# Third feed-forward: ScalarE rounds the gelu rows, VectorE takes the low part a unit later, the down projection stands three units behind

## The chip, the cores and the metric

The kernel runs on one core of one Trainium2 chip. The metric is the device time of one execution in microseconds (us). PE is the matmul engine TensorE, PEld its weight loads, DVE is VectorE, ACT is ScalarE, POOL is GpSimd, SP is the engine that issues the DMAs.

## The reference

`x` has 64 batches of 128 tokens with 128 features. Four layers follow one another; each adds a cross-attention to a context (16 heads) and then a feed-forward. The change touches the third feed-forward alone, a mixture of 8 experts with capacity, cut here to what is computed:

```python
scores = softmax(xt @ wg); gvals, gidx = top_k(scores, 2)        # 8 experts
gvals = gvals / sum(gvals); keep = (place of the token in its expert's queue) < cap
h = gelu(einsum('ecd,edh->ech', disp, w1) + b1[:, None, :])      # D=128 -> H=512
y = einsum('ech,ehd->ecd', h, w2) + b2[:, None, :]
out = sum over the two experts of y * gval * keep
```

The kernel works it out densely: every token goes through all 8 experts, and each expert's output is multiplied by the token's gate, which is zero where the token isn't routed to it or is over the capacity. 8 experts of 512 hidden features are 32 blocks of 128.

## The kernel before

`gated_outputs_phase` is used twice: with kind "capacity" for the third feed-forward (tiles named f2 in the code; the profile leaves numbers out and writes f_a, f_ah and so on) and with kind "swiglu" for the fourth (f3). The flag `two` is true for the fourth.

The 8192 tokens are worked in 16 groups of 512. In a group there is one unit for each hidden block: N = 32 units in the third feed-forward, so 512 units in the stage. fp32 products are made of three passes over operands split in a high part (fp32r, rounded) and a low part (the rest): high x high, low weight x high, high weight x low. One unit n consists of

- up (TensorE): three 128x512 matmuls of the split inputs `XH`, `XL` into `PU[n % 2]`, counted by `up_ready`. It waits until the gelu of unit n-2 is done (`a_ready` at n-1).
- rows (ScalarE): gelu with bias from `PU` into `A[n % 2]`, counted by `a_ready`. It waits for `up_ready` and for `lo_ready` at n-1, that is for the low part of unit n-2, the last reader of the `A` buffer that it overwrites.
- high: `AH[n % 4]` = `A` rounded to fp32r, counted by `hi_ready`. In the third feed-forward VectorE does it (line 1642), in the fourth ScalarE (line 1734).
- low (VectorE, line 1648): `AL[n % 4]` = `A` - `AH`, counted by `lo_ready`. It waits for `hi_ready` of its own unit.
- down (TensorE): three matmuls of `AH` and `AL` into `PY`, which gathers the four units of an expert. The first unit of an expert also has one bf16 matmul (line 1794) that spreads the gates into `PG`.

For each expert ScalarE copies `PG` to SBUF (spread, line 1749), VectorE weighs the expert's output with it (weigh, line 1663, after the down of the expert's fourth unit), and GpSimd sums the weighed outputs in SBUF (lines 1608 and 1611, 7 sums in a group). Once in a group TensorE turns the sum back and VectorE adds it to `x` and takes statistics (finish, in unit 5), TensorE and ScalarE bring the next group's gates in (unit 8), and VectorE splits the next group's inputs (unit 10, lines 1627 and 1629).

The order on every engine is written out by hand: the `group` function of each engine lists what it does in unit s. `lagged(g, s, first, lag, f)` calls f for the unit that lies `lag` units back, in the group before if need be. The down projection, weigh and spread lie LAG units back; LAG is 2 in the third feed-forward and 3 in the fourth. Engines run their own list in order and meet at semaphores only. The first and the last groups are written out, the others are a loop of two groups (`groups_loop`).

Of the kernel before, what the change touches and what calls it, by code (L numbers as in the profile page):

```python
# [39 lines left out]
def at_least(eng, sem, value):  # L40

    if isinstance(value, int) and value <= 0:
        return
    eng.wait_ge(sem, value)
# [1453 lines left out]
def gated_outputs_phase(nc, R, I, name, kind, out=None):  # L1498
# [7 lines left out]
    HB = 4 if kind == "capacity" else 2  # L1506
    N = E * HB
    two = kind == "swiglu"
    LAG = 3 if two else 2


    SUM_UNIT, TURN_UNIT, SPLIT_UNIT, PRESUM_UNIT = 5, 8, 10, 12
# [2 lines left out]
    with ExitStack() as stack:  # L1515
# [41 lines left out]
        def lagged(g, s, first, lag, f):  # L1557

            if s >= lag:
                f(g, s - lag)  # L1560
            elif not first:
                f(g - 1, N + s - lag)

        with nc.Block() as block:
# [56 lines left out]
            @block.vector  # L1621
            def _(dve):
                v = nc.vector
                def split_inputs(g, par):
                    src = X.ht[:, bass.ds(g * GT, GT)]
                    at_least(dve, Z["up_ready"], (g - 1) * N)
                    v.tensor_copy(XH[par][:], src).then_inc(Z["xh_ready"], 1)
                    dve.wait_ge(Z["xh_ready"], g + 1)
                    v.tensor_tensor(XL[par][:], src, XH[par][:].bitcast(F32), ALU.subtract).then_inc(Z["xl_ready"], 1)

                def product(g, s):
                    n = g * N + s
                    dve.wait_ge(Z["s_ready"], n + 1)
                    dve.wait_ge(Z["up_ready"], n + 1)
                    at_least(dve, Z["lo_ready"], n - 1)
                    v.tensor_tensor(A[s % 2][:], S[s % 2][:], PV[s % 2][:], ALU.mult).then_inc(Z["a_ready"], 1)  # L1636

                def high(g, s):
                    n = g * N + s
                    dve.wait_ge(Z["a_ready"], n + 1)  # L1640
                    at_least(dve, Z["dn_ready"], n - 3)
                    v.tensor_copy(AH[s % 4][:], A[s % 2][:]).then_inc(Z["hi_ready"], 1)  # L1642

                def low(g, s):
                    n = g * N + s
                    dve.wait_ge(Z["hi_ready"], n + 1)
                    at_least(dve, Z["dn_ready"], n - 3)
                    v.tensor_tensor(AL[s % 4][:], A[s % 2][:], AH[s % 4][:].bitcast(F32),  # L1648
                                    ALU.subtract).then_inc(Z["lo_ready"], 1)

                def weigh(g, u):

                    if u % HB != HB - 1:
                        return
                    e = u // HB
                    dve.wait_ge(Z["gx_ready"], g * E + e + 1)
                    dve.wait_ge(Z["dn_ready"], g * N + u + 1)

                    at_least(dve, Z["ya_ready"], g * ADDS + (e - 1 if e < 2 else max(1, e - 2)))
                    if two:  # L1660
                        ins = v.tensor_tensor(YG[e % 2][:], PY[e % 2][:], GX[e % 2][:], ALU.mult)  # L1661
                    else:
                        ins = v.scalar_tensor_tensor(YG[e % 2][:], PY[e % 2][:], B2[:, e:e + 1], GX[e % 2][:], ALU.add, ALU.mult)  # L1663
                    ins.then_inc(Z["yg_ready"], 1)

                def presum(g, par):

                    dve.wait_ge(kept_in[par], ctx_count(g, par))
                    v.tensor_tensor(KEPT[par][:], KEPT[par][:], R.x[:, bass.ds(g * GB, GB), :],
                                    ALU.add).then_inc(Z["presummed"], 1)  # L1670

                def group(g, par, first, last):
                    for s in range(N):
                        if out is not None and s == PRESUM_UNIT:
                            presum(g, par)
                        if two:
                            product(g, s)
                            lagged(g, s, first, 1, low)
                        else:
                            high(g, s)  # L1680
                            low(g, s)
                        lagged(g, s, first, LAG, weigh)
                        if s == SUM_UNIT and not first:
                            finish(g - 1, 1 - par)
                        if s == SPLIT_UNIT and not last:
                            split_inputs(g + 1, 1 - par)
                    if last:
                        if two:
                            low(g, N - 1)
                        for u in range(N - LAG, N):  # L1690
                            weigh(g, u)
                        finish(g, par)

                def finish(g, par):

                    dve.wait_ge(Z["px_ready"], g + 1)
                    if out is not None:
                        dve.wait_ge(Z["presummed"], g + 1)
                        v.tensor_tensor(KEPT[par][:], KEPT[par][:], PT[:], ALU.add).then_inc(Z["x_added"], 1)
                        return  # L1700
                    residual(nc, R, dve, Z["x_added"], g, PT[:], g + 1)

                split_inputs(0, 0)

                v.tensor_copy(g3[:, :, 0, :], X.gates[:]).then_inc(Z["split"], 1)
                dve.wait_ge(Z["split"], 1)
                v.tensor_tensor(rest[:], X.gates[:], g3[:, :, 0, :], ALU.subtract).then_inc(Z["split"], 1)
                dve.wait_ge(Z["split"], 2)
                v.tensor_copy(g3[:, :, 1, :], rest[:]).then_inc(Z["split"], 1)
                dve.wait_ge(Z["split"], 3)  # L1710
                v.tensor_tensor(rest[:], rest[:], g3[:, :, 1, :], ALU.subtract).then_inc(Z["split"], 1)
                dve.wait_ge(Z["split"], 4)
                v.tensor_copy(g3[:, :, 2, :], rest[:]).then_inc(Z["split"], 1)
                groups_loop(dve, group)

            @block.scalar
            def _(act):
                a = nc.scalar

                def rows(g, s):  # L1720
                    n = g * N + s
                    act.wait_ge(Z["up_ready"], n + 1)
                    if two:
                        at_least(act, Z["a_ready"], n - 1)
                        a.activation(S[s % 2][:], PU[s % 2][:], ACT.Silu).then_inc(Z["s_ready"], 1)  # L1725
                    else:
                        at_least(act, Z["lo_ready"], n - 1)
                        a.activation(A[s % 2][:], PU[s % 2][:], ACT.Gelu, bias=B1[:, s:s + 1]).then_inc(Z["a_ready"], 1)  # L1728

                def high(g, s):  # L1730
                    n = g * N + s
                    act.wait_ge(Z["a_ready"], n + 1)
                    at_least(act, Z["dn_ready"], n - 3)
                    a.activation(AH[s % 4][:], A[s % 2][:], ACT.Copy).then_inc(Z["hi_ready"], 1)

                def gates_in(g, par):
                    act.wait_ge(Z["gt_psum"], g + 1)
                    at_least(act, Z["ge_ready"], (g - 1) * E)
                    a.activation(G3T[par][:], PT[0:K3, :, :].rearrange("p b t -> p (b t)"),
                                 ACT.Copy).then_inc(Z["gt_ready"], 1)  # L1740

                def spread(g, u):

                    if u % HB != 0:
                        return
                    e = u // HB
                    act.wait_ge(Z["ge_ready"], g * E + e + 1)
                    at_least(act, Z["yg_ready"], g * E + e - 1)
                    a.activation(GX[e % 2][:], PG[:], ACT.Copy).then_inc(Z["gx_ready"], 1)

                def group(g, par, first, last):
                    for s in range(N):
                        rows(g, s)
                        if two:
                            lagged(g, s, first, 1, high)
                        lagged(g, s, first, LAG, spread)
                        if s == TURN_UNIT and not last:
                            gates_in(g + 1, 1 - par)
                    if last:
                        if two:  # L1760
                            high(g, N - 1)
                        for u in range(N - LAG, N):
                            spread(g, u)

                gates_in(0, 0)
                groups_loop(act, group)
# [187 lines left out]
```

## Time and profile before

| | us |
|---|---|
| median of 3 runs (4551.13 to 4552.9) | 4552.88 |
| span of the profiled execution, first to last instruction | 4550.5 |
| TensorE busy in it | 4085.3 |
| VectorE busy | 3902.8 |
| ScalarE busy | 2713.1 |
| GpSimd busy | 1476.4 |

The profiled execution has no other time of its own on record than its span; it lies 2.4 us under the median of the timed runs. The third feed-forward is the stretch from about 1995 us to 2812 us. Its steady part, 2050 to 2750 us, holds TensorE at full granted clock. A matmul's busy time overlaps that of the next one, since they are pipelined: their starts, not their durations, give the cadence. Instructions of VectorE and ScalarE that don't depend on each other also overlap by about 0.1 us.

### The profile page before, as it was taken

What the parts mean: (1) busy time and instruction counts of PE and PEld (TensorE: products, weight loads), DVE (VectorE), ACT (ScalarE), POOL (GpSimd) and SP (SyncE); (2) the same over time, 40 slices, a digit from 0 to 9 for tenths busy, and PEclk for the clock granted to TensorE, in tenths of its full rate; (3) what the DMA queues carried; (4) which work ended last, traced back from release to release, by engine and by line L of the source; (5) the groups of instructions that cost most, each with busy time, mean ns of one, the idle gap of its engine ahead of it and who ended that gap; (6) DMA issues with size and microseconds to landing.
All of it is one profiled execution on the core that took longest, in us unless ns stands there. A gap on an engine that the chain in (4) does not pass through costs nothing. (4 is left out here: it accounts for less than half of the span.)

```text
span 4550.5 us, 105158 instructions
## 1 busy us (share of the span) xinstructions
PE 4085.3 (90%) x34134; PEld 2858.5 (63%) x34135; DVE 3902.8 (86%) x7025; ACT 2713.1 (60%) x4836; POOL 1476.4 (32%) x779
## 2 busy tenths in 40 slices
PE   6984789994997999869999997999949999699999
PEld 3562556664774666657777775666636666577777
DVE  7888789997996888779999998888868888688888
ACT  3433577772775777535555554777757777366665
POOL 2210055540004555312111213555525555122222
PEclk9976999995998999869999998999969999699999
DMA  1010022221002222200000000222222221100000
GB/s 59 17 46 1 11 68 63 65 49 49 1 0 57 57 59 58 78 24 1 1 0 1 0 1 23 64 55 60 52 64 47 55 50 47 72 15 14 14 14 14
DMA packets 129636, 162.04 MB, mean 36 GB/s; under 512 B 32972, under 2 KB 88593, under 8 KB 128306
## 3 DMA queue, kind: packets, MB, share of 16 engines
q1 hardware_dynamic: 129457, 159.97, 13.3%
q8 instruction: 75, 1.23, 0.1%
q14 instruction: 104, 0.84, 0.1%
HBM read 36.38 MB, written 8.39 MB: 10 GB/s over the span
## 5 line engine op out<-in xcount | busy, mean ns | idle before, releaser
L709 ACT ACTIVATE a_p<-a_p 128x480 f32<-128x480 f32 x832 | 500.7, 602 | 408.0 <-DVE a_p L551 403.8
L1648 DVE TENSOR_TENSOR f_al<-f_a,f_ah 128x512 fp32r<-128x512 f32 x768 | 690.9, 900 | 17.5
L347 POOL TENSOR_TENSOR a_km<-a_k,a_slots 96x1920 fp32r<-96x1920 f32 x186 | 631.8, 3416 | 180.8 <-DMA a_k<-a_kh 180.8
L546 DVE TENSOR_REDUCE a_mx<-a_sc 128x4 f32<-128x480 f32 (+1 forms) x832 | 543.0, 653 | 140.0 <-PE a_sc L802 108.2
L1728 ACT ACTIVATE f_a<-f_pu,f_b 128x512 f32<-128x512 f32 x512 | 353.4, 690 | 374.1 <-PE f_pu L1231 198.6
L551 DVE TENSOR_TENSOR a_p<-a_sc,a_mx 128x480 f32<-128x480 f32 x832 | 531.8, 639 | 18.8
L715 ACT ACTIVATE a_pt<-a_tp 120x512 f32<-120x512 f32 x832 | 486.4, 585 | 76.3 <-PE a_tp L811 73.8
L811 PE MATMUL a_tp<-ident,a_p 128*120 128x128 f32 x3328 | 511.8, 276 | 12.0 <-ACT a_p L709 9.7
L1611 POOL TENSOR_TENSOR f_ya<-f_ya,f_yg 128x512 f32<-128x512 f32 x192 | 254.0, 1323 | 769.1 <-DVE f_yg L1663 466.6
L811 PEld LDWEIGHTS a_tp<-ident,a_p 128*120 128x120 f32 x3328 | 400.3, 138 | 98.8 <-ACT a_p L709 34.8
L796 PE MATMUL a_sc<-a_km,a_qr 96*128 96x480 f32 x768 | 396.2, 516 | 33.0 <-ACT a_qr L704 31.4
L1227 PE MATMUL f_py<-f_ah,f_wdhi 128*128 128x512 f32 x768 | 355.2, 462 | 3.0 <-DVE f_ah L1642 3.0
L835 PE MATMUL a_nd<-a_pt,a_vm 120*32 120x128 f32 x6656 | 354.9, 285 | 0.0
L835 PE MATMUL a_nd<-a_pt,a_dm 120*32 120x128 f32 x6656 | 334.4, 273 | 0.0
L1231 PE MATMUL f_py<-f_al,f_wdhi 128*128 128x512 f32 x768 | 312.6, 407 | 6.2 <-DVE f_al L1648 4.4
L1227 PE MATMUL f_pu<-f_xh,f_w1hi 128*128 128x512 f32 x768 | 310.8, 405 | 3.6 <-DVE f_a L1636 3.5
L1228 PE MATMUL f_py<-f_ah,f_wdlo 128*128 128x512 f32 x768 | 303.3, 395 | 0.0
L1228 PE MATMUL f_pu<-f_xh,f_w1lo 128*128 128x512 f32 x768 | 303.2, 395 | 0.0
L1231 PE MATMUL f_pu<-f_xl,f_w1hi 128*128 128x512 f32 x768 | 302.6, 394 | 0.0
L1725 ACT ACTIVATE f_s<-f_pu 128x512 f32<-128x512 f32 x256 | 153.5, 600 | 212.6 <-PE f_pv L1231 212.6
L559 DVE RECIPROCAL a_rd<-a_nd 128x128 f32<-128x128 f32 x256 | 242.8, 948 | 6.7 <-PE a_nd L835 6.5
L347 POOL TENSOR_TENSOR s_km<-s_k,s_slots 96x2048 fp32r<-96x2048 f32 x62 | 223.9, 3631 | 53.0 <-DMA s_k<-s_kh 53.0
(403 smaller groups left out, 9394.3 us busy)
## 6 DMA issues: line engine op xcount, KB each, us to landing
a_q<-a_qh SPq DMA_DIRECT2D x384, 64.0 KB, 2.0
a_k<-a_kh SPq DMA_DIRECT2D x384, 60.0 KB, 2.0
a_ctx<-in_ctxT SPq DMA_DIRECT2D x64, 240.0 KB, 2.7
a_q<-a_ql SPq DMA_DIRECT2D x192, 64.0 KB, 2.0
a_k<-a_kl SPq DMA_DIRECT2D x192, 60.0 KB, 2.0
s_k<-s_kh SPq DMA_DIRECT2D x128, 64.0 KB, 2.0
s_q<-s_qh SPq DMA_DIRECT2D x128, 64.0 KB, 2.0
x<-in_x SPq DMA_DIRECT2D x4, 1024.0 KB, 7.9
```

The costliest lines, as they stand in the source:

```text
L347: v.tensor_tensor(KM[par][:, i, :, :].rearrange("p b (j k) -> p b j k", k=KN), K3[:, i, :, :].unsqueeze(2).to_broadcast([TR, GB, 4, KN]), ...
L546: v.tensor_reduce(mx[:], view, AX.X, ALU.max).then_inc(mx_ready, 1)
L551: v.tensor_tensor(PR[s % 4][:].rearrange("p (h k) -> p h k", k=k), view, mx[:].unsqueeze(2).to_broadcast([P, heads, k]), ALU.subtract).the ...
L709: a.activation(PR[s % 4][:], PR[s % 4][:], ACT.Exp).then_inc(exp_ready, 1)
L715: a.activation(PT[s % 4][0:KN, :], TP[s % 2][0:KN, :], ACT.Copy).then_inc(pt_ready, 1)
L796: last = t.matmul(SC[s % 2][:, 0:W], queries, keys, start=True, stop=not masked)
L811: last = t.transpose(TP[s % 2][0:KN, q * P:(q + 1) * P], PR[s % 4][:, q * KN:(q + 1) * KN], R.ident[:])
L835: last = t.matmul(ND[j % 2][32 * q:32 * q + 32, what, :], w, PT[s % 4][0:KN, q * P:(q + 1) * P], start=(what == 0 and i == 0), stop=(i == ...
L1227: t.matmul(out, w_hi, a_hi, start=start, stop=False)
L1228: t.matmul(out, w_lo, a_hi, start=False, stop=False)
L1231: return t.matmul(out, w_hi, a_lo, start=False, stop=stop)
L1648: v.tensor_tensor(AL[s % 4][:], A[s % 2][:], AH[s % 4][:].bitcast(F32), ALU.subtract).then_inc(Z["lo_ready"], 1)
```

## The change

In the third feed-forward the high part is taken by ScalarE, one unit after the gelu, in place of VectorE; the low part on VectorE moves one unit back; and LAG becomes 3, so down, weigh and spread lie three units back. The conditions on semaphores stay as they are, and so do the numbers of buffers: `A` has 2, `AH` and `AL` have 4. The fourth feed-forward had this order already.

```diff
--- before.py
+++ after.py
@@ -1506,7 +1506,7 @@
     HB = 4 if kind == "capacity" else 2
     N = E * HB
     two = kind == "swiglu"
-    LAG = 3 if two else 2
+    LAG = 3
 
 
     SUM_UNIT, TURN_UNIT, SPLIT_UNIT, PRESUM_UNIT = 5, 8, 10, 12
@@ -1635,12 +1635,6 @@
                     at_least(dve, Z["lo_ready"], n - 1)
                     v.tensor_tensor(A[s % 2][:], S[s % 2][:], PV[s % 2][:], ALU.mult).then_inc(Z["a_ready"], 1)
 
-                def high(g, s):
-                    n = g * N + s
-                    dve.wait_ge(Z["a_ready"], n + 1)
-                    at_least(dve, Z["dn_ready"], n - 3)
-                    v.tensor_copy(AH[s % 4][:], A[s % 2][:]).then_inc(Z["hi_ready"], 1)
-
                 def low(g, s):
                     n = g * N + s
                     dve.wait_ge(Z["hi_ready"], n + 1)
@@ -1675,18 +1669,14 @@
                             presum(g, par)
                         if two:
                             product(g, s)
-                            lagged(g, s, first, 1, low)
-                        else:
-                            high(g, s)
-                            low(g, s)
+                        lagged(g, s, first, 1, low)
                         lagged(g, s, first, LAG, weigh)
                         if s == SUM_UNIT and not first:
                             finish(g - 1, 1 - par)
                         if s == SPLIT_UNIT and not last:
                             split_inputs(g + 1, 1 - par)
                     if last:
-                        if two:
-                            low(g, N - 1)
+                        low(g, N - 1)
                         for u in range(N - LAG, N):
                             weigh(g, u)
                         finish(g, par)
@@ -1751,14 +1741,12 @@
                 def group(g, par, first, last):
                     for s in range(N):
                         rows(g, s)
-                        if two:
-                            lagged(g, s, first, 1, high)
+                        lagged(g, s, first, 1, high)
                         lagged(g, s, first, LAG, spread)
                         if s == TURN_UNIT and not last:
                             gates_in(g + 1, 1 - par)
                     if last:
-                        if two:
-                            high(g, N - 1)
+                        high(g, N - 1)
                         for u in range(N - LAG, N):
                             spread(g, u)
```

How the instructions stand. On ScalarE at the start of the stage, before (f2_a0 and f2_a1 are the two buffers of gelu rows, f2_pu the up projection's, f2_gx the spread gates):

```order
L1728 ACTIVATE f2_a0<-f2_pu0,f2_b1 128x512
L1728 ACTIVATE f2_a1<-f2_pu1,f2_b1 128x512
L1728 ACTIVATE f2_a0<-f2_pu0,f2_b1 128x512
L1749 ACTIVATE f2_gx0<-f2_pg 128x512
L1728 ACTIVATE f2_a1<-f2_pu1,f2_b1 128x512
L1728 ACTIVATE f2_a0<-f2_pu0,f2_b1 128x512
L1728 ACTIVATE f2_a1<-f2_pu1,f2_b1 128x512
L1728 ACTIVATE f2_a0<-f2_pu0,f2_b1 128x512
```

and in the changed kernel (f2_ah0 to f2_ah3 are the high parts):

```order
L1718 ACTIVATE f2_a0<-f2_pu0,f2_b1 128x512
L1718 ACTIVATE f2_a1<-f2_pu1,f2_b1 128x512
L1724 ACTIVATE f2_ah0<-f2_a0 128x512
L1718 ACTIVATE f2_a0<-f2_pu0,f2_b1 128x512
L1724 ACTIVATE f2_ah1<-f2_a1 128x512
L1718 ACTIVATE f2_a1<-f2_pu1,f2_b1 128x512
L1724 ACTIVATE f2_ah2<-f2_a0 128x512
L1739 ACTIVATE f2_gx0<-f2_pg 128x512
L1718 ACTIVATE f2_a0<-f2_pu0,f2_b1 128x512
L1724 ACTIVATE f2_ah3<-f2_a1 128x512
```

After the first two gelus each gelu has the rounding of the unit before behind it: the gelu into f2_a0 of unit 2 now stands right behind the rounding that reads f2_a0 of unit 0.

On VectorE at the same place, before (f2_al are the low parts, f2_yg the weighed output):

```order
L1642 CAST f2_ah2<-f2_a0 128x512
L1648 TENSOR_TENSOR f2_al2<-f2_a0,f2_ah2 128x512
L1642 CAST f2_ah3<-f2_a1 128x512
L1648 TENSOR_TENSOR f2_al3<-f2_a1,f2_ah3 128x512
L1642 CAST f2_ah0<-f2_a0 128x512
L1648 TENSOR_TENSOR f2_al0<-f2_a0,f2_ah0 128x512
L1642 CAST f2_ah1<-f2_a1 128x512
L1648 TENSOR_TENSOR f2_al1<-f2_a1,f2_ah1 128x512
L1663 SCALAR_TENSOR_TENSOR f2_yg0<-f2_py0,f2_b2,f2_gx0 128x512
L1642 CAST f2_ah2<-f2_a0 128x512
```

and in the changed kernel:

```order
L1642 TENSOR_TENSOR f2_al2<-f2_a0,f2_ah2 128x512
L1642 TENSOR_TENSOR f2_al3<-f2_a1,f2_ah3 128x512
L1642 TENSOR_TENSOR f2_al0<-f2_a0,f2_ah0 128x512
L1642 TENSOR_TENSOR f2_al1<-f2_a1,f2_ah1 128x512
L1657 SCALAR_TENSOR_TENSOR f2_yg0<-f2_py0,f2_b2,f2_gx0 128x512
L1642 TENSOR_TENSOR f2_al2<-f2_a0,f2_ah2 128x512
```

The casts are gone from VectorE, and between two weighings four low parts are left; the weighing of expert 0 comes one unit later.

## Rows read from the trace of the kernel before

**Rows 1.** the page, part 1: busy us, share of span, x instructions
```profile
PE 4085.3 (90%) x34134; PEld 2858.5 (63%) x34135; DVE 3902.8 (86%) x7025; ACT 2713.1 (60%) x4836; POOL 1476.4 (32%) x779
```

**Rows 2.** busy time by engine in a steady stretch of the changed stage
```profile
core 0: us, PE busy (x) PEld busy (x) DVE busy (x) ACT busy (x) POOL busy (x), PEclk, DMA share, GB/s
2050.00:2750.00 700.00, 682.26 (x2881) 501.90 (x2880) 662.75 (x1097) 368.08 (x568) 138.25 (x110) 1.00 0.00 1
```

**Rows 3.** groups by line, same stretch: busy us, mean ns, idle before, releaser
```profile
L1648 DVE TENSOR_TENSOR f_al<-f_a,f_ah 128x512 fp32r<-128x512 f32 x444 | 400.9, 903 | 15.2
L1728 ACT ACTIVATE f_a<-f_pu,f_b 128x512 f32<-128x512 f32 x443 | 305.8, 690 | 329.2 <-PE f_pu L1231 169.2 <-DVE f_al L1648 158.1
...
L1642 DVE CAST f_ah<-f_a 128x512 fp32r<-128x512 f32 x444 | 187.6, 423 | 19.5 <-issue 14.8 <-ACT f_a L1728 4.5
...
L1611 POOL TENSOR_TENSOR f_ya<-f_ya,f_yg 128x512 f32<-128x512 f32 x82 | 109.7, 1338 | 403.9 <-DVE f_yg L1663 403.9
```

**Rows 4.** who waited for whom, same stretch: us total, times, longest
```profile
ACT f_a L1728 <- DVE f_al L1648: 158.1, 130, 2.9
...
PEld f_py L1231 <- DVE f_al L1648: 43.3, 124, 1.1
```

**Rows 5.** timeline of ACT, the stage's first and last gelu instructions
```profile
2000.77 1.28 ACT L1728 ACT_TABLE_LOAD   x1
2002.07 1.34 ACT L1728 ACTIVATE f_a<-f_pu,f_b 128x512 f32<-128x512 f32 x2
...
2803.85 0.69 ACT L1728 ACTIVATE f_a<-f_pu,f_b 128x512 f32<-128x512 f32 x1 [0.46 <-PE f_pu L1231]
```

**Rows 6.** timeline, DVE, ACT and POOL around one sum of outputs
```profile
2305.31 0.69 ACT L1728 ACTIVATE f_a<-f_pu,f_b 128x512 f32<-128x512 f32 x1 [0.71 <-PE f_pu L1231]
...
2305.79 0.75 DVE L1663 SCALAR_TENSOR_TENSOR f_yg<-f_py,f_b,f_gx 128x512 f32<-128x512 f32 x1
...
2305.90 0.59 ACT L1749 ACTIVATE f_gx<-f_pg 128x512 f32<-128x512 f32 x1
...
2306.45 0.42 DVE L1642 CAST f_ah<-f_a 128x512 fp32r<-128x512 f32 x1
...
2306.70 1.32 POOL L1611 TENSOR_TENSOR f_ya<-f_ya,f_yg 128x512 f32<-128x512 f32 x1 [4.63 <-DVE f_yg L1663]
...
2306.91 1.67 DVE L1648 TENSOR_TENSOR f_al<-f_a,f_ah 128x512 fp32r<-128x512 f32 x1
...
2308.67 0.69 ACT L1728 ACTIVATE f_a<-f_pu,f_b 128x512 f32<-128x512 f32 x1 [1.04 <-DVE f_al L1648]
...
2309.01 0.69 DVE L1648 TENSOR_TENSOR f_al<-f_a,f_ah 128x512 fp32r<-128x512 f32 x1
...
2309.62 0.42 DVE L1642 CAST f_ah<-f_a 128x512 fp32r<-128x512 f32 x1
```

**Rows 7.** groups by line, the fourth feed-forward: ScalarE's rounding
```profile
L1734 ACT ACTIVATE f_ah<-f_a 128x512 fp32r<-128x512 f32 x256 | 159.6, 623 | 3.8 <-DVE f_a L1636 3.8
```

**Rows 8.** timeline, a VectorE instruction released by ScalarE
```profile
2317.03 0.69 ACT L1728 ACTIVATE f_a<-f_pu,f_b 128x512 f32<-128x512 f32 x1
...
2317.75 0.43 DVE L1642 CAST f_ah<-f_a 128x512 fp32r<-128x512 f32 x1 [0.32 <-ACT f_a L1728]
```

**Rows 9.** timeline of PE, the cadence of back-to-back matmuls
```profile
2304.42 0.39 PE L1227 MATMUL f_pu<-f_xh,f_w1hi 128*128 128x512 f32 x1
2304.65 0.40 PE L1228 MATMUL f_pu<-f_xh,f_w1lo 128*128 128x512 f32 x1
```

**Rows 10.** timeline of DVE, residual and statistics, then the next unit
```profile
2312.41 0.68 DVE L154 TENSOR_TENSOR x<-x,f_pt 128x512 f32 x1
...
2314.16 0.41 DVE L1642 CAST f_ah<-f_a 128x512 fp32r<-128x512 f32 x1
```

**Rows 11.** PE busy us and granted clock, 1 us stretches, first attention
```profile
180.00:181.00 1.00, 0.00 (x0) 1.00 0.00 0
182.00:183.00 1.00, 1.00 (x5) 0.50 0.00 0
```

## The prediction

> **What bounds the kernel now.** I read the page's sum first, then the busy times of the stage that changes, its groups by line, its waits, and last a few microseconds of its timeline. The page shows TensorE busy for 90% of the span and VectorE for 86% [rows 1]; that is a mean over all stages. In 700 us of the third feed-forward TensorE is busy 682.26 us and VectorE 662.75 us, both nearly full, ScalarE only 368.08 us, at full granted clock [rows 2]. One VectorE unit is a cast of 423 ns and a low part of 903 ns on average [rows 3]; one TensorE unit is six matmuls that start 0.23 us apart, 1.40 us [rows 9]. The pace of the stage: the first gelu starts at 2002.07, the last, 511 units later, at 2803.85 [rows 5], so 801.8 us, or 1.57 us a unit. TensorE is the bound most of the time, and its weight load for the low part's pass waits 43.3 us in all for VectorE [rows 4]. By busy shares alone, moving a cast from a 95% engine to a 53% engine looks like a gain. What decides is another row: already now the gelu (ScalarE, line 1728) stands idle 158.1 us, 130 times, until a low part is done [rows 4]. The gelu of unit n may not overwrite `A[n % 2]` before the low part of unit n-2 has been taken from it, since there are two `A` buffers. That wait stays, and the change lengthens what hangs on it.
>
> **The change, part by part.**
>
> The cast leaves VectorE: 512 casts of 423 ns, 217 us of work [rows 3]. A rounding of the same size enters ScalarE; the fourth feed-forward has that instruction at 623 ns [rows 7], 319 us of work. As load this would fit: ScalarE would have 0.59 us for the gelu (0.69 less 0.10 of overlap), 0.52 for the rounding (0.62 less the same), and a spread for every fourth unit.
>
> The ring is the point. ScalarE's list is now gelu n, rounding n-1, gelu n+1, rounding n, and so on. Gelu n+1 waits for low part n-1, low part n-1 waits for rounding n-1, and rounding n-1 stands on ScalarE directly ahead of gelu n+1. Nothing of the low part can lie beside ScalarE's work any more except a spread. Before, cast and low part of unit n-1 both ran on VectorE while ScalarE was free to do gelu n. So one unit of the changed kernel is this chain, in order:
>
> - gelu starts, the next independent instruction on ScalarE starts 0.59 us later (2305.31 to 2305.90) [rows 6];
> - the rounding, 0.62 us [rows 7];
> - from ScalarE's end to VectorE's start 0.03 us (2317.03 + 0.69 to 2317.75) [rows 8];
> - the low part, 0.69 us when nothing blocks it (the row at 2309.01) [rows 6];
> - from its end to the gelu's start 0.09 us (2306.91 + 1.67 = 2308.58 to 2308.67) [rows 6].
>
> Together 2.02 us, with the unrounded 623 and 693 ns 2.03 us. The spread hides: it starts 0.5 us after the rounding's start and lasts 0.59, while rounding, hop and low part take 1.34. TensorE hides wholly: it needs 1.40 us a unit (and a little for the gates), it may start up n+2 once gelu n is done, and down stands three units back, so nobody waits for it. LAG 3 therefore buys nothing here and costs nothing: on VectorE a weighing starts right behind a low part, 0.61 us after that low part's start (2309.01 to 2309.62) [rows 6], and is over before ScalarE has done gelu and rounding.
>
> The GpSimd sums. After a weighing GpSimd sums SBUF tiles for 1.32 us, beginning 0.91 us after the weighing began (2305.79 to 2306.70); the low part that meets it lasts 1.67 us in place of 0.69 and ends 0.56 us after the sum's end (2308.02 to 2308.58) [rows 6]. In the new order, with t the start of the low part ahead of the weighing: weighing t+0.61, sum t+1.52 to t+2.84, next low part ready at t+2.03 and done at t+2.84+0.56 = t+3.40 rather than t+2.72. So each sum costs the ring 0.68 us. There are 7 in each of 16 groups, 112. Bounds: nothing, if the low part came first and the sum had to wait; 0.98 us each (1.67 - 0.69), if the whole lengthening of the row shows. I take 0.68, being the arithmetic of the same rows with the new distances.
>
> The Trainium skill ("SBUF — State Buffer", "Who interferes with whom") says that a VectorE instruction with two SBUF inputs contends with a GpSimd instruction that reads SBUF, and that ScalarE never waits on anyone. The trace agrees with the first part: 1.67 against 0.69 us [rows 6]. By that rule the rounding on ScalarE is safe from the sums, and the low part stays exposed.
>
> Once a group. Finish in unit 5 holds VectorE for 1.75 us (2312.41 to 2314.16) [rows 10]; it starts at t+0.61, so the next low part starts at t+2.36 and not t+2.03: 0.33 us, 15 times. The split of inputs in unit 10 now stands behind a weighing, because LAG 3 brings one there: cast and subtraction follow it, the subtraction meets the GpSimd sum, and the low part behind it ends about 0.6 us later than a plain blocked one (its own 0.69, overlapped by 0.09), 15 times. No table is loaded again: the only ACT_TABLE_LOAD here is at the start of the stage [rows 5], though gelus and copies alternate already.
>
> The stage's end: before, two whole downs were left behind the last gelu, now part of three, but the weighing waits for the last low part in both; I cost it at nothing.
>
> The sum: 511 x 2.03 = 1037.3; 112 x 0.68 = 76.2; 15 x 0.33 = 5.0; 15 x 0.6 = 9.0; together 1127.5 us against 801.8 now, that is +325.7 us. The span of 4550.5 becomes 4876.2, and the profiled execution lies 2.4 us under the median of the timed runs, so on the median of 4552.88 the forecast is 4878 us, 7.2% slower.
>
> **The rivals.**
>
> *Slow clock in the gaps.* TensorE will work 1.40 us and stand for 0.63 us in every unit (1.3 us where a sum blocks). If the granted clock falls to its lower level in such gaps, a unit of matmuls costs up to 2.8 us, more than the ring's mean of 1127.5 / 511 = 2.21 us. For it: in the first attention TensorE idles from 180 to 181 us with the clock at 1.00, and from 182 to 183 us, busy again, it has 0.50 [rows 11]. Against it: the gaps here are mostly shorter than that whole idle microsecond, and at the low clock TensorE would have no gap left, so that it would be busy throughout and the clock could not stay down. At worst I let half the units run so: 256 x (2.8 - 2.21) = 151, 5029 us. The Trainium skill ("TensorE: Matmul & The Clock Gate", "A second HAM failure mode: psum-queue depth-cycling") holds that micro-idles between matmul groups make the clock swing between its levels; that speaks for this rival, and no stretch of this trace has such short gaps in every unit to test it.
>
> *Faster: relief of VectorE wins.* Then a unit would go at TensorE's pace. For it: the 95% busy VectorE, and the 43.3 us for which TensorE's weight loads wait [rows 2, 4]. The price: at most 43.3 x 809 / 700 = 50 us, for 809 us of stage, giving 4503; at least the 17.74 us that TensorE is idle in 700, so 20. The point from which it decides is the ring's length: it must be under 1.57 us, and that needs a gelu which doesn't wait for the low part behind the rounding just issued. Two rows alone, rounding 0.62 and low part 0.69, with 0.59 for the gelu, are already 1.90.
>
> *The sums block longer.* All of 0.98 us each: 112 x 0.30 = 34 more, 4912. *The sums don't block:* 76 less, 4802. The row at 1.67 speaks against the second.
>
> *Smaller handovers.* 0.03 us from VectorE to ScalarE in place of 0.09: 31 less, 4847.
>
> **How the numbers follow.** The ring holds with a chance of 0.96: 0.76 near my sum, 0.08 with longer blocks, 0.05 with no blocks or smaller handovers, 0.07 with the clock falling often enough to be seen. Relief of VectorE gets 0.03, no difference 0.01. The range, 4835 to 4930, reaches from a little below the smaller handovers to above the longer blocks with a few falls of the clock. A measurement of this kernel tells 0.2%, 9 us, from no change: slower 0.96, same 0.01, faster 0.03.
>
> **What would show it.** Right: the gelu's wait for the low part rises from 158 us to most of ScalarE's idle time and happens in nearly every unit; gelu starts 2.03 us apart, about 2.7 behind a sum; the rounding at 0.62 us; waits of TensorE are for the gelu, no longer for the low part; the stage lasts some 1135 us with TensorE busy about two thirds, at granted clock 1.0; all other stages unchanged. Wrong: gelu starts less than 1.57 us apart (the ring isn't one), a granted clock under 1.0 inside the stage, or low parts that last 0.69 us in every unit (the sums don't block).

## The result, and the profile after

The changed kernel takes 4873.81 us (median, 4869.67 to 4874.8) against 4552.62 us: ratio 1.0705, 95% interval 1.0692 to 1.0718. The forecast was 4878, in a range of 4835 to 4930. The profiled execution took 4869.67 us, the shortest of the four, so what follows from the trace is about 4 us less than the medians say.

Part 1 of the page of the changed kernel, beside [rows 1]:

```profile
PE 4241.6 (87%) x34134; PEld 2832.8 (58%) x34135; DVE 3686.0 (76%) x6513; ACT 2974.6 (61%) x5348; POOL 1470.9 (30%) x779
```

VectorE has 512 instructions less and 217 us less work, as counted; ScalarE has 512 more and 262 us more work. VectorE lost load and the time went up all the same, so VectorE's load is not what sets it; that ScalarE's isn't either is shown by e1 and e9 below. The stage that changed, in a steady stretch, beside [rows 2], and the fourth feed-forward, which has the same order and didn't change:

```profile
core 0: us, PE busy (x) PEld busy (x) DVE busy (x) ACT busy (x) POOL busy (x), PEclk, DMA share, GB/s
2050.00:3050.00 1000.00, 841.17 (x2958) 493.55 (x2957) 489.94 (x666) 611.31 (x1039) 138.97 (x114) 1.00 0.00 0
2005.00:3120.00 1115.00, 938.75 (x3299) 550.57 (x3297) 544.53 (x741) 682.29 (x1159) 152.49 (x124) 1.00 0.00 0
4300.00:4800.00 500.00, 496.74 (x2215) 386.11 (x2214) 439.53 (x610) 311.26 (x568) 135.69 (x111) 1.00 0.05 14
```

VectorE falls from 95% to 49% busy, TensorE from 97% to 84% by records that overlap (by starts it has 1.40 us of matmuls in 2.19 us, 64%), and the clock is granted in full. In the fourth feed-forward (last row) TensorE stays full with the rounding in the same place: there ScalarE's activation goes to a buffer `S` of its own, which is free once VectorE's product has read it, ahead of the rounding and not behind it. That reason is read from the code; no run tests it. The groups by line of the same 1000 us, beside [rows 3] (busy us, mean ns, then idle time before them and its releaser):

```profile
L1642 DVE TENSOR_TENSOR f_al<-f_a,f_ah 128x512 fp32r<-128x512 f32 x455 | 367.1, 807 | 506.7 <-ACT f_ah L1724 506.7
L1718 ACT ACTIVATE f_a<-f_pu,f_b 128x512 f32<-128x512 f32 x455 | 312.7, 687 | 388.7 <-DVE f_al L1642 388.7
L1724 ACT ACTIVATE f_ah<-f_a 128x512 fp32r<-128x512 f32 x456 | 283.4, 621 | 0.0
...
L1611 POOL TENSOR_TENSOR f_ya<-f_ya,f_yg 128x512 f32<-128x512 f32 x86 | 111.0, 1290 | 650.4 <-DVE f_yg L1657 650.4
```

Each of the 455 gelus now waits for a low part, and 427 of the 455 low parts wait for a rounding: the two idle columns, 388.7 and 506.7 us, are the two halves of the ring. The rounding itself never waits. The waits of the same stretch, beside [rows 4]:

```profile
ACT f_a L1718 <- DVE f_al L1642: 388.7, 455, 1.6
PEld f_pu L1227 <- ACT f_a L1718: 245.8, 420, 0.6
...
PEld f_py L1231 <- DVE f_al L1642: 159.8, 334, 1.5
```

TensorE's weight loads wait for the gelu 420 times, and for the low part 334 times. One of these gaps, in its timeline:

```profile
2307.49 0.47 PE L1231 MATMUL f_py<-f_al,f_wdhi 128*128 128x512 f32 x1
2308.24 0.50 PE L1227 MATMUL f_pu<-f_xh,f_w1hi 128*128 128x512 f32 x1 [0.28 <-ACT f_a L1718]
```

Matmuls otherwise start 0.23 us apart, so about 0.5 us of this unit is empty. The ring itself, in the timeline of ScalarE and VectorE (start us, duration us, engine, line):

```profile
2307.51 0.69 ACT L1718 ACTIVATE f_a<-f_pu,f_b 128x512 f32<-128x512 f32 x1 [0.82 <-DVE f_al L1642]
2308.09 0.62 ACT L1724 ACTIVATE f_ah<-f_a 128x512 fp32r<-128x512 f32 x1
2309.53 0.69 ACT L1718 ACTIVATE f_a<-f_pu,f_b 128x512 f32<-128x512 f32 x1 [0.82 <-DVE f_al L1642]
2310.12 0.62 ACT L1724 ACTIVATE f_ah<-f_a 128x512 fp32r<-128x512 f32 x1
2311.56 0.69 ACT L1718 ACTIVATE f_a<-f_pu,f_b 128x512 f32<-128x512 f32 x1 [0.82 <-DVE f_al L1642]
...
2314.23 0.69 ACT L1718 ACTIVATE f_a<-f_pu,f_b 128x512 f32<-128x512 f32 x1 [0.98 <-DVE f_al L1642]
```

```profile
2308.74 0.69 DVE L1642 TENSOR_TENSOR f_al<-f_a,f_ah 128x512 fp32r<-128x512 f32 x1 [1.33 <-ACT f_ah L1724]
2310.77 0.69 DVE L1642 TENSOR_TENSOR f_al<-f_a,f_ah 128x512 fp32r<-128x512 f32 x1 [1.33 <-ACT f_ah L1724]
2311.38 0.74 DVE L1657 SCALAR_TENSOR_TENSOR f_yg<-f_py,f_b,f_gx 128x512 f32<-128x512 f32 x1
2312.80 1.34 DVE L1642 TENSOR_TENSOR f_al<-f_a,f_ah 128x512 fp32r<-128x512 f32 x1 [0.67 <-ACT f_ah L1724]
```

```profile
2312.29 1.29 POOL L1611 TENSOR_TENSOR f_ya<-f_ya,f_yg 128x512 f32<-128x512 f32 x1 [8.06 <-DVE f_yg L1657]
```

Gelu at 2307.51, rounding 0.58 us later at 2308.09, its end at 2308.71, low part from 2308.74 to 2309.43, next gelu at 2309.53: 2.02 us, link by link as forecast. At 2311.56 the same chain meets a GpSimd sum: the low part lasts 1.34 us, and the next gelu comes after 2.67 us.

### The profile page after: what moved, and what is told of

Its sections match the earlier page's. It is cut to its first block and busy times, and to the rows that moved or that the text cites. A ratio compares the mean times of both kernels' runs of the same rounds, so it can differ in the third digit from the quotient of the medians.

```text
span 4867.9 us, 105172 instructions
## 1 busy us (share of the span) xinstructions
PE 4241.6 (87%) x34134; PEld 2832.8 (58%) x34135; DVE 3686.0 (76%) x6513; ACT 2974.6 (61%) x5348; POOL 1470.9 (30%) x779
## 5 line engine op out<-in xcount | busy, mean ns | idle before, releaser
L1642 DVE TENSOR_TENSOR f_al<-f_a,f_ah 128x512 fp32r<-128x512 f32 x768 | 641.4, 835 | 575.1 <-ACT f_ah L1724 575.1
L1724 ACT ACTIVATE f_ah<-f_a 128x512 fp32r<-128x512 f32 x768 | 477.8, 622 | 3.9 <-DVE f_a L1636 3.9
L1227 PE MATMUL f_pu<-f_xh,f_w1hi 128*128 128x512 f32 x768 | 360.4, 469 | 120.3 <-ACT f_a L1718 102.8
L1231 PE MATMUL f_py<-f_al,f_wdhi 128*128 128x512 f32 x768 | 335.2, 436 | 59.5 <-DVE f_al L1642 57.7
L1227 PEld LDWEIGHTS f_pu<-f_xh,f_w1hi 128*128 128x128 f32 x768 | 144.2, 188 | 303.2 <-ACT f_a L1718 276.1
```

The lines of the kernel that those rows point to most:

```text
L1227: t.matmul(out, w_hi, a_hi, start=start, stop=False)
L1231: return t.matmul(out, w_hi, a_lo, start=False, stop=stop)
```

## The experiments

All edits are in the third feed-forward only, and the diffs show the lines that matter; `...` stands for lines left out. Times are medians, and ratios are to the kernel before on the same chip. It took 4552.09 to 4552.99 us on all of them, so the runs can also be held against the changed kernel's 4873.81.

**Cut the ring: four buffers of gelu rows (e1).**

```diff
-        A = [sb(n_(f"a{i}"), [P, GT]) for i in range(2)]
+        NA = 2 if two else 4
+        A = [sb(n_(f"a{i}"), [P, GT]) for i in range(NA)]
...
-                        at_least(act, Z["lo_ready"], n - 1)
+                        at_least(act, Z["lo_ready"], n - NA + 1)
...
```

> The changed kernel with four buffers of gelu rows instead of two, so that the gelu of unit n waits for the low part of unit n-4 and not of unit n-2; the order on every engine is the changed one. Ring theory: the chain gelu, rounding, low part, gelu is cut, ScalarE needs 0.59 + 0.52 + 0.5/4 = 1.24 us a unit, VectorE about 1.15, TensorE 1.40 and its gates, so TensorE sets the pace: about 4505 us, between 4495 and 4540. Rival, ScalarE's own load is what costs: stays near 4870. Rival, LAG 3 or the clock in the gaps: stays above 4800.

Measured 4535.62 us, ratio 0.9967 (0.9954 to 0.9979): within the range given, 31 us over the 4505 expected. With ScalarE's and VectorE's lists unchanged, 338 us come back for two buffers. The groups by line of 650 us of the stage:

```profile
L1719 ACT ACTIVATE f_a<-f_pu,f_b 128x512 f32<-128x512 f32 x420 | 289.6, 690 | 93.3 <-PE f_pu L1231 70.2 <-issue 20.6
L1725 ACT ACTIVATE f_ah<-f_a 128x512 fp32r<-128x512 f32 x420 | 261.1, 622 | 0.0
```

The gelu's idle time is now for TensorE, except for 20.6 us "issue", to which the last two runs return. ScalarE's load is as in the changed kernel, so it was not the load.

**Cut the ring by order alone: rounding behind its own gelu (e4).** Two buffers, three units behind; ScalarE's list is gelu n, rounding n, and VectorE takes the low part of unit n in its own step.

```diff
-                        lagged(g, s, first, 1, high)
+                        lagged(g, s, first, 1 if two else 0, high)
...
-                        lagged(g, s, first, 1, low)
+                        lagged(g, s, first, 1 if two else 0, low)
```

> The changed kernel, still two buffers and ScalarE rounding, but the rounding stands right behind the gelu of its own unit and the low part is not put back a unit. Ring theory: the low part of unit n-1 now runs beside gelu and rounding of unit n, so ScalarE needs about 0.72 + 0.52 + 0.5/4 = 1.37 us a unit and TensorE sets the pace: 4500 to 4540 us. Rival, ScalarE's load costs: no better than 4870. Rival, LAG 3: above 4800.

Measured 4510.92 us, ratio 0.9911 (0.9894 to 0.9927), the fastest of all and faster than both kernels. In it the low part of unit n-1 has all of gelu and rounding n to run beside. Busy times of 650 us of the stage:

```profile
2050.00:2700.00 650.00, 650.00 (x2840) 505.48 (x2839) 415.71 (x643) 607.83 (x996) 163.53 (x110) 1.00 0.00 0
```

TensorE has no idle in the records; the gelu's starts put a group at 47.67 us (759.1 us for 511 units, 1.49 a unit), 1.40 us of matmuls a unit and the gates' and transposes' share. As far as the records show, the order of the other engines has nothing more to give here.

**LAG alone, both ways (e2, e3).** e2 is the changed kernel with `LAG = 3 if two else 2`; e3 is the kernel before with `LAG = 3`.

> The changed kernel with down projection, weighing and spread two units behind instead of three. Ring theory: the ring is the same, 2.03 us a unit; only the split of inputs no longer stands behind a weighing, 15 times 0.6 = 9 us less: about 4865 us. Rival, three units behind is what costs: back near 4553 us.

> The kernel before with the down projection, weighing and spread three units behind instead of two, rounding still on VectorE. Ring theory: nothing is in the ring that was not there; TensorE's waits for the low part (43 us in 700) shrink, the split of inputs meets a GpSimd sum: 4520 to 4560 us. Rival, three units behind is what costs: above 4800 us.

Measured 4869.66 us for e2 (ratio to before 1.07, 1.0682 to 1.0718) and 4538.8 us for e3 (0.9972, 0.9961 to 0.9983). Three units behind costs nothing; in the kernel before it gains 13 us. The waits of e3 in 650 us:

```profile
ACT f_a L1728 <- DVE f_al L1648: 292.4, 314, 2.9
...
PEld f_py L1231 <- DVE f_al L1648: 5.6, 13, 0.4
```

TensorE waits 5.6 us for the low part, where the kernel before has 40.5 in the same 650 us. Not all of the gain is this. By the gelu starts the stage is 14 us shorter: most groups last 49.0 us and not 49.5, and in every other group VectorE's idle at the top of its loop (see the last two runs) falls from 2.5 to 1.4 us, which gives 6 of the 14.

e2 lies 4 us under the changed kernel where 9 were expected, and by its gelu starts only 0.8 us (1118.0 against 1118.8). The unit with the split of inputs is back at 2.02 us and the sum there costs the unit before it its 0.6 us, so the split gives back the expected 0.7 us a group; but now finish stands behind a weighing and its unit takes 2.98 us in place of 2.33, which takes the same away.

**One link shortened: half a low part (e8).** The subtraction covers 256 of 512 columns; the other half of `AL` is written once at the start.

```diff
-                    v.tensor_tensor(AL[s % 4][:], A[s % 2][:], AH[s % 4][:].bitcast(F32),
+                    W = GT if two else 256
+                    v.tensor_tensor(AL[s % 4][:, 0:W], A[s % 2][:, 0:W], AH[s % 4][:, 0:W].bitcast(F32),
...
```

> The changed kernel whose low part in the third feed-forward covers 256 of the 512 columns (the other half keeps what was written once at the start), all else as it is. Ring theory: the low part is a link of the ring, so its shortening by an estimated 0.27 us (from 0.69) comes back in each of 512 units: 137 us less, about 4737 us. Rival, the cost is ScalarE's load or TensorE's gaps: VectorE is idle half the time already, so no change, 4874.

Measured 4736.62 us (ratio 1.041, 1.0393 to 1.0427), 137 us under the changed kernel. One instruction of an engine that is idle half the time became 0.27 us shorter, and every unit with it. Its timeline:

```profile
2304.64 0.69 ACT L1723 ACTIVATE f_a<-f_pu,f_b 128x512 f32<-128x512 f32 x1 [0.55 <-PE f_pu L1231]
...
2306.40 0.69 ACT L1723 ACTIVATE f_a<-f_pu,f_b 128x512 f32<-128x512 f32 x1 [0.55 <-DVE f_al L1643]
```

```profile
2305.88 0.42 DVE L1643 TENSOR_TENSOR f_al<-f_a,f_ah 128x256 fp32r<-128x256 f32 x1 [1.33 <-ACT f_ah L1729]
```

1.76 us from gelu to gelu, with a low part of 0.42 us.

**Work beside the ring shortened: a spread of 64 columns (e9).**

```diff
-                    a.activation(GX[e % 2][:], PG[:], ACT.Copy).then_inc(Z["gx_ready"], 1)
+                    W = GT if two else 64
+                    a.activation(GX[e % 2][:, 0:W], PG[:, 0:W], ACT.Copy).then_inc(Z["gx_ready"], 1)
...
```

> The changed kernel whose spread on ScalarE covers 64 of 512 columns (the rest keeps what was written once), so that ScalarE has about 0.4 us less work in 128 places, 50 us. Ring theory: the spread lies beside rounding and low part, so nothing comes back: 4874, within 9. Rival, ScalarE's load is what costs: 40 to 50 us less, about 4828.

Measured 4872.43 us (1.0707, 1.0689 to 1.0725). The spread lasts 0.21 us in place of 0.59 in 128 places, and nothing comes back:

```profile
L1740 ACT ACTIVATE f_gx<-f_pg 128x64 f32<-128x64 f32 x74 | 15.9, 214 | 0.0
```

e8 and e9 are the pair that tells a ring from a load: the instruction on the less busy engine counted in full, the one on the busier engine not at all.

**The sums: 64 of 512 columns (e5).** Both additions of GpSimd on `YA[par][:, 0:64]`.

> The changed kernel whose GpSimd sums in the third feed-forward cover 64 of 512 columns, so that they last a small part of 1.3 us. Ring theory with blocking: 112 units lose their 0.62 us, and the split of inputs its 0.6, 15 times: 78 us less, about 4796 us. If the sums don't block the low part: 4874.

Measured 4796.75 us (1.0538, 1.052 to 1.0555): 77 us less by the medians, 72 by the gelu starts of the two traces (1046.6 against 1118.8). The low part and the sum:

```profile
L1644 DVE TENSOR_TENSOR f_al<-f_a,f_ah 128x512 fp32r<-128x512 f32 x317 | 219.2, 692 | 352.2 <-ACT f_ah L1726 352.2
...
L1613 POOL TENSOR_TENSOR f_ya<-f_ya,f_yg 128x64 f32<-128x64 f32 x59 | 18.9, 320 | 463.3 <-DVE f_yg L1659 463.3
```

The mean low part is 692 ns, where the changed kernel has 807; none is blocked any more.

**The kernel before with four buffers (e6).** The edit of e1, with the cast left on VectorE.

> The kernel before with four buffers of gelu rows, rounding still on VectorE and down two units behind. In the kernel before the gelu waited 158 us in 700 for a low part, but TensorE waited only 43 us for VectorE, and VectorE is 95% busy: the gelu's waits go, VectorE's load stays. Expected 4545 us, between 4520 and 4555. If the gelu's wait was what held TensorE: 4505.

Measured 4553.42 us (1.0003, 0.9993 to 1.0013): no change. The gelu's waits for the low part are gone from its trace and have become waits for TensorE (289.2 us, 398 times, in 650); TensorE's own wait for the low part is the old one:

```profile
ACT f_a L1729 <- PE f_pu L1231: 289.2, 398, 1.6
...
PEld f_py L1231 <- DVE f_al L1649: 41.0, 115, 1.1
```

So two buffers were enough for the old order. With ScalarE rounding they are enough too, if the rounding stands right behind its own gelu (e4); they are too few when it stands a unit later, directly ahead of the gelu that waits for its low part.

**The top of the loop (e10, e11).** In e1 every other group lasted 51.7 us by its gelu starts, the others 47.5. The gelu at the top of ScalarE's loop of two groups starts late, with no releaser:

```profile
2144.10 0.59 ACT L1740 ACTIVATE f_gx<-f_pg 128x512 f32<-128x512 f32 x1
2148.30 0.69 ACT L1719 ACTIVATE f_a<-f_pu,f_b 128x512 f32<-128x512 f32 x1 [3.62 <-issue]
```

e10 is e1 with ScalarE's list written out for 16 groups, e11 the kernel before with VectorE's list written out:

```diff
-                groups_loop(act, group)
+                if two:
+                    groups_loop(act, group)
+                else:
+                    for g in range(NG):
+                        group(g, g % 2, g == 0, g == NG - 1)
```

> The kernel with four buffers of gelu rows (run e1), with ScalarE's list of the third feed-forward written out for all 16 groups instead of a loop of two groups; the other engines keep their loops. In run e1 ScalarE stood 3.3 to 3.6 us with no releaser at the top of its loop, once per two groups, and every other group lasted 51.7 us in place of 47.5. If the jump back is what costs: 6 or 7 times 4 us, 25 us less, about 4511 us, as run e4. If it is something else in that place, such as the wait for a group's first inputs: 4535 us as before.

> The kernel before with VectorE's list of the third feed-forward written out for all 16 groups. In its trace every other group lasts 52.0 us in place of 49.5, and VectorE has six idles without a releaser, 14.8 us in 700. If the jump back costs: 6 or 7 times 2.5 us, about 17 us less, 4536 us. If not: 4552 us.

Measured 4522.12 us for e10 (0.9935, 0.9921 to 0.9948) and 4533.12 us for e11 (0.9957, 0.9943 to 0.997). The idles are gone in both, and every group of e10 but the first and the last lasts 48.3 us. e11 gains 20 us where 17 were expected. e10 gains 13 of 25 (17 by the gelu starts), because 25 was too much to expect: the groups of 47.5 us in e1 were not undisturbed ones but followed a stall, of which they made up 0.8 us. An undisturbed group lasts 48.3 us in e1 too (its second), so six jumps cost 2.5 us each, 15 in all. What still parts e10 from e4 is a smaller wait once in each group, TensorE's for a low part. e1 has it too, e4 doesn't:

```profile
PEld f_py L1231 <- DVE f_al L1643: 11.9, 14, 0.9
```

A group of e10 lasts 0.67 us more than one of e4, 11 us in all. The loop alone doesn't make the stall: ScalarE runs the same loop of two groups in the changed kernel and in e4, and has no such idle in either. Its longest there are 1.61 us and 1.08 us, both behind the split of inputs and for a low part.

## Why the prediction was right

*The ring.* Right, and shown from three sides: cut by buffers (e1), cut by order (e4), shortened in one link (e8, 137 us returned of 137 expected). The unit without a sum takes 2.02 to 2.03 us from gelu to gelu; the forecast was 2.03.

*The sums.* Sized 0.68 us; the gelu starts show 0.61 on average, mostly 0.64 and in the first and last groups 0.55. 0.03 of the difference is the sum's own length, now 1290 ns and not 1320. The forecast also charged 112 sums, where two come after the last gelu. e5 gives the whole term: 72 us by the gelu starts (77 by the medians) where 78 were expected of the split and 112 sums; of the split's 0.64 us only half came back.

*Once a group.* The unit of finish takes 2.33 us on average (+0.30; forecast +0.33), the unit behind the split of inputs 3.29 us (+0.64 over a blocked one; forecast +0.6).

*The sum.* From the first gelu at 2000.94 to the last at 3119.75 there are 1118.8 us, forecast 1127.5. The sums account for the 8.7 us: 110 at 0.61 make 67 and not 76. The ring's 2.025 us in place of 2.03 take 2 more off; against them stand 3 us that the forecast doesn't have, since the first three units of a group take 0.04 to 0.08 us longer, for a cause that stays open. On the medians the forecast is 4 us over. That so many small terms come out within a few us of each other is in part luck; that the ring makes up 1035 of 1118.8 us is not.

*LAG 3 costs and buys nothing.* The cost was right (e2, e3), and nobody waits for the down projection in the trace. One detail failed: TensorE was to wait for the gelu and no longer for the low part. It waits for both: TensorE runs two units ahead of ScalarE, so three units behind its own up projection is one unit behind the gelu, and the third pass comes just as the low part ends. It costs nothing, because the ring sets the pace. In the order of the kernel before LAG 3 would have been worth 13 us (e3). And the sign "TensorE busy about two thirds" holds by the starts of its matmuls (64%), not by the profile's busy share, which was 84%.

*The clock.* The rival with the lower clock didn't happen: TensorE stood about 0.5 us in a unit, longer behind a sum, and the granted clock was 1.00 from 2005 to 3120 us. What the Trainium skill says under "A second HAM failure mode: psum-queue depth-cycling", in "TensorE: Matmul & The Clock Gate", that frequent micro-idles between groups of matmuls make the clock swing, isn't borne out here.

*Relief of VectorE.* The rival had the right price for the wrong kernel: 4503 forecast for TensorE's pace, 4510.92 measured in e4, where the rounding on ScalarE is kept and the ring is not. That is in part luck: the price was made of TensorE's waits for the low part, but VectorE's stalls at the top of its loop, which the prediction doesn't name and e4 doesn't have, are alone worth 20 us of the kernel before (e11).

## What to carry to other kernels

When an instruction moves to another engine, follow the buffer it reads back to the engine that fills it: if filler, mover and last reader now stand in a circle, with the mover directly ahead of the next filling in one engine's list, their durations and handovers add up to the pace of a unit, however idle the engines look. Before buying buffers, try the order: the rounding behind its own gelu cost no memory and gave 41 us against the kernel before, with LAG 3 in it. And a wait of 130 times 1.2 us on an engine that is half idle costs nothing by itself (e6), but it names the link that a change must not lengthen.

## What the runs showed of the hardware

- At the jump back to the top of a loop of two groups (64 units) an engine can stall with no releaser: 3.3 to 3.6 us on ScalarE, six times (e1), and 2.4 to 2.6 us on VectorE, six times, in the kernel before, 20 us of its time (e11). Written out, the stalls are gone (e10, e11). But the same loop on ScalarE shows none in the changed kernel and none in e4, where ScalarE is 94% busy. What it takes beside the jump stays open.
- When a low part on VectorE and a sum on GpSimd meet, which of the two is held up depends on the order of starts. In the changed kernel the low part starts 0.51 us after the sum and lasts 1.34 us, the sum 1.29. In e4 the low part starts first, as at 2335.16, and keeps its 0.69 us; the sum lasts 1.74, and 1666 ns on average:

```profile
2335.16 0.69 DVE L1642 TENSOR_TENSOR f_al<-f_a,f_ah 128x512 fp32r<-128x512 f32 x1
...
2335.26 1.74 POOL L1611 TENSOR_TENSOR f_ya<-f_ya,f_yg 128x512 f32<-128x512 f32 x1 [4.12 <-DVE f_yg L1657]
```

```profile
L1642 DVE TENSOR_TENSOR f_al<-f_a,f_ah 128x512 fp32r<-128x512 f32 x436 | 299.7, 690 | 231.9 <-ACT f_ah L1725 230.6
...
L1611 POOL TENSOR_TENSOR f_ya<-f_ya,f_yg 128x512 f32<-128x512 f32 x82 | 136.6, 1666 | 349.1 <-DVE f_yg L1657 349.1
```

The Trainium skill ("SBUF — State Buffer", "Who interferes with whom") says that the order of issue decides which of the two blocks. The trace agrees: started second, the low part lasts 1.34 us and not 0.69, and started second, the sum lasts 1.74 us and not 1.29. But the second doesn't begin its whole work behind the first: the low part ends 0.56 us after the sum and not 0.69, the sum 1.15 us after the low part and not 1.29.
